# Two attention layers with a feed-forward on one core: another order of transposes in three places, weight pieces split earlier, and query and key tiles issued from ScalarE's queue

## The reference

```
layer 0:  q = x Wq^T, k = ctx Wk^T, v = ctx Wv^T
          att = softmax(q k^T / sqrt(32)) v
          x = x + att[0]                 # sequence 0 alone, added to all eight
layer 1:  xq = layer_norm(x), y = layer_norm(ctx)
          o = softmax(q k^T / sqrt(32)) v     # q from xq; k, v from y
          x = x + o Wproj + bproj
          h = gelu(layer_norm(x) W1 + b1)     # 512 -> 2048
          x = x + h W2 + b2
```

## Time and profile before

| | us |
|---|---|
| median of 3 runs (lowest, highest) | 1790.82 (1788.2, 1792.63) |
| profiled execution | 1793.32 |
| its span | 1791.5 |
| first score matmul of layer 1's passes: second, third, fourth | 490.3, 641.9, 806.5 |
| last product with values of the eighth pass begins the tail | 1626.4 |

### The profile page before, as it was taken

How to read it: one execution, slowest core, us unless ns; L and a number is a source line. 1 busy time by engine, 2 the same in 40 slices (tenths; PEclk the granted TensorE clock), 3 DMA queues, 4 the chain that set the end, 5 groups by cost and what they waited for, 6 DMA issues and landing times.

```text
span 1791.5 us, 23794 instructions
## 1 busy us (share of the span) xinstructions
PE 1714.7 (96%) x7456; PEld 1313.6 (73%) x7456; DVE 1082.1 (60%) x1865; ACT 1156.1 (65%) x1940; POOL 939.3 (52%) x802
## 2 busy tenths in 40 slices
PE   7899998998989999999999999999999999999999
PEld 5677776765666777777777777777777777777787
DVE  5565654477776666665666665666656666654322
ACT  4777764587877765765766577657657665775231
POOL 0444455157675564656465564646664655646341
PEclk9999999999999999999999999999999999999999
DMA  8789978674545675676676566756766775668262
GB/s 285 251 278 302 330 275 322 229 213 164 188 132 162 184 201 138 179 235 162 160 219 195 143 168 185 200 133 179 235 168 157 219 197 142 171 185 274 93 234 79
DMA packets 160077, 356.78 MB, mean 199 GB/s; under 512 B 29392, under 2 KB 50000, under 8 KB 159312
## 3 DMA queue, kind: packets, MB, share of 16 engines
q1 hardware_dynamic: 109072, 189.31, 35.8%
q10 hardware_dynamic: 50880, 165.95, 29.5%
HBM read 253.61 MB, written 82.08 MB: 187 GB/s over the span
## 4 chain that ended last, share of the span: by engine, by line
PE 69%; ACT 8%; DMA 7%; DVE 5%; issue 4%; POOL 3%; SPq 2%; ACTq 0%; DVEq 0%; POOLq 0%
PE ps_d L887 46%; PE ps_o L908 11%; PE ps_t L940 6%; PE ps_s L925 5%; DMA q_st<-negmax_t 3%; ACT p_hi L1054 2%; DVE negmax L1212 1%; DMA rs<-o_raw 1%; ACT ps_d L960 1%; ACT ps_t L1061 1%; ACT ht L1016 1%; POOL p_lo L1324 1%; SPq L728 1%; PE ps_d L815 1%; DMA v_scratch<-v_out 1%
## 5 line engine op out<-in xcount | busy, mean ns | idle before, releaser
L1324 POOL TENSOR_TENSOR p_lo<-p_full,p_hi 128x512 fp32r<-128x512 f32 x288 | 372.1, 1292 | 586.5 <-ACT p_full L1061 586.0
L1054 ACT ACTIVATE p_hi<-ps_t 128x512 fp32r<-128x512 f32 x576 | 345.7, 600 | 358.5 <-PE ps_t L940 355.0
L1212 DVE TENSOR_REDUCE negmax<-ps_s 128x1 fp32r<-128x512 f32 x576 | 388.9, 679 | 128.2 <-PE ps_s L925 127.6
L887 PE MATMUL ps_d<-hT,w_r 128*128 128x512 f32 x1536 | 419.0, 393 | 2.0 <-DVE hT L1109 2.0
L887 PE MATMUL ps_d<-w_r,g_s 128*128 128x512 f32 x1536 | 389.4, 393 | 0.0
L887 PEld LDWEIGHTS ps_d<-hT,w_r 128*128 128x128 f32 x1536 | 288.6, 189 | 73.7 <-DVE hT L1109 5.7
L887 PEld LDWEIGHTS ps_d<-w_r,g_s 128*128 128x128 f32 x1536 | 290.3, 189 | 64.6
L1225 DVE TENSOR_TENSOR p_lo<-ps_t,p_hi 128x512 fp32r<-128x512 f32 x288 | 198.8, 690 | 229.9 <-ACT ps_t L1061 229.2
L908 PE MATMUL ps_o<-p_hi,v_s 128*65 128x512 f32 x576 | 231.5, 402 | 14.7 <-POOL p_lo L1324 8.1
L940 PE MATMUL ps_t<-q_st,k_st 97*128 97x512 f32 x576 | 232.2, 403 | 11.6 <-DMA q_st<-negmax_t 10.9
L925 PE MATMUL ps_s<-k_st,q_st 96*128 96x512 f32 x576 | 231.8, 402 | 8.4 <-DVE negmax L1212 6.6
(11 more groups left out here) (102 smaller groups left out, 2160.6 us busy)
## 6 DMA issues: line engine op xcount, KB each, us to landing
w_r<-w_scratch ACTq DMA_DIRECT2D x214, 512.0 KB, 5.3
w_r<-w_scratch SPq DMA_DIRECT2D x42, 512.0 KB, 4.7
v_scratch<-v_out SPq DMA_DIRECT2D x36, 520.0 KB, 5.2
k_scratch<-kq_out SPq DMA_DIRECT2D x36, 512.0 KB, 4.9
q_st<-q_scratch SPq DMA_DIRECT2D x144, 128.0 KB, 4.5
k_st<-k_scratch SPq DMA_DIRECT2D x144, 128.0 KB, 4.3
o_ab<-o_raw SPq DMA_DIRECT2D x144, 128.0 KB, 3.5
w_scratch<-piece_out SPq DMA_DIRECT2D x16, 1024.0 KB, 6.4
```

Source lines behind the costliest of these rows:

```text
L887: ins = nc.tensor.matmul(bank(u), lhs[a], rhs[b], start=(i == 0 and m == 0), stop=(i == 3 and m == 2))
L1054: act.activation(p_hi[:, c], ps_t[:, c % 2], ACT.Exp, scale=SCALE)
L1212: dve.tensor_reduce(negmax[:, h % 2, c:c + 1], ps_s[:, c % 2], AX.X, ALU.max, negate=True).then_inc(s_maxed, 1)
L1324: pool.tensor_tensor(p_lo[:, c], p_full[:, (by_gpsimd(s) - 1) % 2], p_hi[:, c].bitcast(F32), ALU.subtract).then_inc(p_pool_split, 1)
```

## The change

- `keys_values` gives the same units in another order: the transposes of the next sequence come between the keys and values two at a time, and all of them ahead of the last value and the last key with its value. This holds in the first pass and in the gap.
- In the tail, the last `y2` unit of the sequence before goes ahead of the four `ht` transposes, where it stood between the second and the third.
- In the later passes the two `y2` units behind the second Gelu burst get three ticks of their own (25 to 27), and the four `ht` transposes with the hidden units the twelve after them, where all were spread over fifteen.
- The eight pieces of W2 are loaded, split and stored six ticks earlier.
- From tick `base[2]` on, ScalarE issues the heads' query and key tiles (after the exponentials and the emptying of its tick), SyncE no longer does. The waits ahead of them are the same.

```diff
--- before.py
+++ after.py
@@ -113,10 +113,9 @@
 
         def keys_values(b):
             units = []
-            for c in range(4):
-                units += [("k", b + 1, c), ("v", b + 1, c)]
-                if b + 1 < B:
-                    units.append(("a", 3 + b, c))
+            turns = [("a", 3 + b, c) for c in range(FC) if b + 1 < B]
+            units = [("k", b + 1, 0), ("v", b + 1, 0), *turns[:1], ("k", b + 1, 1), *turns[1:2], ("v", b + 1, 1), *turns[2:3],
+                     ("k", b + 1, 2), *turns[3:], ("v", b + 1, 2), ("k", b + 1, 3), ("v", b + 1, 3)]
             return units
 
         early = [("a", 2, c) for c in range(FC)]
@@ -174,8 +173,8 @@
                 spread([drain + 1], second(old, 2)[2:], front=True)
                 spread([drain + 2], second(old, 3)[:1], front=True)
                 spread([drain + 3], outs, front=True)
-                spread([drain + 4], second(old, 3)[1:3], front=True)
-                spread([drain + 5], turns[:2] + second(old, 3)[3:] + turns[2:], front=True)
+                spread([drain + 4], second(old, 3)[1:], front=True)
+                spread([drain + 5], turns, front=True)
                 spread([drain + 6], hidden(new, 0), front=True)
                 by_chunk(drain + 6, new, 0)
                 spread([drain + 7], hidden(new, 1), front=True)
@@ -197,7 +196,8 @@
                 spread(range(at + 22, at + 24), hidden(old, 3)[3:])
                 burst(at + 24, old, 3, second(old, 2)[:2])
                 rest = second(old, 2)[2:]
-                spread(range(at + 25, at + 40), rest + turns + hidden(new, 0))
+                spread(range(at + 25, at + 28), rest)
+                spread(range(at + 28, at + 40), turns + hidden(new, 0))
                 burst(at + 40, new, 0, second(old, 3)[:2])
                 spread(range(at + 41, at + 55), second(old, 3)[2:] + hidden(new, 1))
             else:
@@ -328,7 +328,7 @@
 
 
 def piece_tick(i):
-    return PRE + 19 + 5 * i if i < PIECES // 2 else PLAN.gap - 11 + 2 * (i - PIECES // 2)
+    return PRE + 19 + 5 * i if i < PIECES // 2 else PLAN.gap - 17 + 2 * (i - PIECES // 2)
 
 
 PIECE_SPLIT = listed([(piece_tick(i), i) for i in range(PIECES)])
@@ -369,6 +369,7 @@
 
 
 SHARED_FROM = PLAN.base[1] + 2
+STACKS_FROM = PLAN.base[2]
 
 HEADS, ROWS, PLACES, VALUES, STORES, STAGE_LOADS, RES_LOADS, OUT_STORES = sync_tables()
 
@@ -698,6 +699,22 @@
         queue.wait_ge(evacuated, ready("y2", n, 12 + t))
         queue.dma_start(rows(out, n - 1)[:, t], xres[n % 2][:, t]).then_inc(out_stored[n % 2], 16)
 
+    def load_stack(queue, h):
+        n, g, k = h // NH, h % NH // G, h % G
+        own = slice(h % NH * DK, h % NH * DK + DK)
+        if h >= G:
+            queue.wait_ge(t_ready, (h - G) * TC + TC)
+        elif h == 0:
+            queue.wait_ge(first_split["ctx0t"], FC)
+        if k == 0:
+            for u in (("k", n, g), ("q", n, g)):
+                i = KQ_NO[u]
+                queue.wait_ge(kq_stored[i % 2], 16 * (i // 2 + 1))
+        k_hi = kd[n, own, 0].unsqueeze(1).broadcast_to([DK, 2, T])
+        for dst, src in ((q_st[0:2 * DK, k], qd[n, own]), (k_st[0:2 * DK, k], k_hi),
+                         (q_st[2 * DK:KQ, k], qd[n, own, 0]), (k_st[2 * DK:KQ, k], kd[n, own, 1])):
+            queue.dma_start(dst.bitcast(F32), src).then_inc(stack_loaded[k], 16)
+
     def load_wo(queue):
         queue.wait_ge(unit_ready, ready("a", 10, FC - 1))
         queue.dma_start(wo_raw[:], wo).then_inc(wo_loaded, 16)
@@ -706,22 +723,6 @@
 
     @block.sync
     def _(sp):
-        def load_stack(h):
-            n, g, k = h // NH, h % NH // G, h % G
-            own = slice(h % NH * DK, h % NH * DK + DK)
-            if h >= G:
-                sp.wait_ge(t_ready, (h - G) * TC + TC)
-            elif h == 0:
-                sp.wait_ge(first_split["ctx0t"], FC)
-            if k == 0:
-                for u in (("k", n, g), ("q", n, g)):
-                    i = KQ_NO[u]
-                    sp.wait_ge(kq_stored[i % 2], 16 * (i // 2 + 1))
-            k_hi = kd[n, own, 0].unsqueeze(1).broadcast_to([DK, 2, T])
-            for dst, src in ((q_st[0:2 * DK, k], qd[n, own]), (k_st[0:2 * DK, k], k_hi),
-                             (q_st[2 * DK:KQ, k], qd[n, own, 0]), (k_st[2 * DK:KQ, k], kd[n, own, 1])):
-                sp.dma_start(dst.bitcast(F32), src).then_inc(stack_loaded[k], 16)
-
         def load_row(h):
             sp.wait_ge(max_turned, h + 1)
             for c in range(TC):
@@ -777,8 +778,8 @@
             early = tick < SHARED_FROM
             for u in STORES.get(tick, []) if early else ():
                 store(sp, *u)
-            for h in HEADS.get(tick, []):
-                load_stack(h)
+            for h in HEADS.get(tick, []) if tick < STACKS_FROM else ():
+                load_stack(sp, h)
             for h in PLACES.get(tick, []):
                 place_head(h)
             for n, g in VALUES.get(tick, []) if early else ():
@@ -1063,6 +1064,8 @@
                 move_head(weighted // TC)
             for u in EVACUATED.get((tick, True), []):
                 evacuate(*u)
+            for h in HEADS.get(tick, []) if tick >= STACKS_FROM else ():
+                load_stack(act, h)
             for n, group, c in G_HALVES.get(tick, []):
                 done = GELU_NO[n, group]
                 if (n, group) in PLAN.by_chunk.get(tick, []):
```

## The result

The change makes the kernel slower: 1814.6 us median (1813.54 to 1816.09) beside 1791.72 for the kernel before on the same chip, a ratio of 1.0108 (95% interval 1.0086 to 1.0131), or +19.4 us (15.4 to 23.5). The two medians lie 22.9 us apart; the ratio, with its interval, is what is used here. The forecast was 1783.4, faster, within 1774 to 1793.

A forecast was written before the change was run, and what follows sets the result against it. TensorE was taken as the bound, working 1714.7 of 1791.5 us, leaving 77 us to win. The terms summed to -7.4 us: 1785.9 for the profiled execution, 1783.4 against the median, range 1774 to 1793.

The forecast's parts named there:

- ScalarE issues the tiles: From head 34 on: issues hidden under ScalarE's exponentials, +1 us where ScalarE is full (490 to 520), bounds 0 and 8.
- the rival of ScalarE's sequencer: After Gelu bursts and at third pass's start: four issues push the next exponential, holding matmuls; +5.6 us, 1796, chance 0.07.
- Rows: SyncE's row copies no longer stand behind the tiles: -2 of their 3.2 us of waits, bounds -3.2 and +3.
- The queues hold each other up: Rival: SyncE's row issues wait for ScalarE's, rows come 2 us later; +8.6 us, 1799, chance 0.04.
- Turns: Later passes: transposes' wait goes, but ScalarE's emptying delays hidden units and splits; +0.5 a pass, +3 us, bounds -7.6 and +8.
- Pieces: W2 pieces six ticks earlier: gain at most 2.27 us, loss at most 4.5 from late splits; taken as +0.5.
- Terms (a) to (c): Gap: wait at 275.78 shortened, -1.5 and -0.7; wait at 309.37 gone, -6.4; new accumulator-reuse waits, +1.5; together -7.1 us.
- (c): Gap: value units reuse a chunk's accumulator after one large unit, waiting half a us and about 1 us; +1.5, bounds 0 and 2.9.
- the rival of the gain given back: Second layer reached 7 us sooner, but SyncE's queue or stores there set the pace; -0.3 us, 1790.5, chance 0.22.
- First pass and tail: First pass: 1.81 us wait at 137.98 goes, -1.8; tail: last output unit ahead of transposes, -1, bounds -3 and +1.7.

The follow-up runs named there:

- the issues alone: The kernel before with ScalarE issuing the query and key tiles from the second pass of the second layer on, nothing else: ratio 1.0098, +17.6 us.
- the turns alone: The kernel before with the two output units ahead of the transposes in the later passes, nothing else: ratio 1.0039, +7.0 us.
- two issues moved: The kernel before with ScalarE issuing the query tiles alone, two DMAs a head; SyncE keeps the key tiles: ratio 0.9985, -2.7 us.
- the four copies: The kernel before with ScalarE additionally issuing four 2 KB copies a head that nothing reads; SyncE keeps the tiles: ratio 1.0172, +31 us.
- the new order and tail: The kernel before with the new order of keys, values and transposes and the new tail, without the other three edits: ratio 0.9958, -7.5 us.
- the row early: The kernel before with new key order and tail, plus SyncE issuing the first pass's last head's output and row-of-sums copies two ticks earlier: ratio 0.9937.
- the pieces early: The kernel before with the last eight pieces of W2 six ticks earlier, nothing else: ratio 1.0018, +3.2 us.

## Why the prediction was wrong

**The step that failed** is "ScalarE issues the tiles", with its "hidden" and +1 us; issues and rows together measured +17.6 in place of -1. Its mechanism was written down as the rival of ScalarE's sequencer, but with a chance of 0.07, and mis-sized twice. The issue was priced at 0.33 to 0.51 us from one row each; the trace of before already had 0.58 and 0.60 us as medians of its 576 tile issues on SyncE, and on ScalarE four took 2.35 us with no pause (914.60). And that was held against the average distance of two exponentials, 2.5 us. By that measure 2.35 us would still have been hidden, so the price alone was not what failed. A tick's ScalarE work is not its two exponentials: the parts of the Gelu stand behind the issues in the same tick, `o_raw` in the next one, and other issues (weights, x) as well; at 807.61 six of them last 3.6 us. The row at the earlier trace rows, one issue of 0.33 us under one exponential, was read as proof for four. The rival's bounds (16 heads, six bursts) gave 1796; instead every pass from the third on lost 2.2 to 3.6 us with the issues alone. Two of the signs that the prediction named for being wrong came: an exponential behind the issues starts late (811.30), and the late passes are longer by more than 1.5 us.

**Rows.** -2 was forecast for SyncE's rows. Their wait, 3.2 us before, is 2.2 in the kernel after and 1.2 with the issues alone, but 1.9 with the turns alone too, where SyncE kept the tiles: what the term is worth is not shown. With two issues moved, the kernel is 2.7 us faster, not told apart from none.

**The queues hold each other up.** No support: the waits for the rows did not grow where ScalarE issues four in a tick (2.2, 1.2, and 3.0 with the four copies, against 3.2), and SyncE's four row issues beside ScalarE's took 2.2 us at 808.17 and at 914.96, as at the earlier trace rows.

**Turns.** +3 forecast, with bounds of -7.6 and +8; +7.0 (3.8 to 10) measured. That the wait would not go but move, to the hidden unit and the other transposes, was right; 0.5 us a pass was too little.

**Pieces.** +0.5 forecast, up to 4.5; +3.2 (0.2 to 6.5) measured. What was named as late next, the deviation on GpSimd and ScalarE's scaling behind it, is what the trace shows at 238.83 and 240.60. Missing was the row of sums in the crowded queue.

**The gap.** Terms (a) to (c) came to -7.1. The waits named did shrink or go: in the kernel after 309.37 is gone, the third transpose's went from 2.03 to 1.63. What failed, by the profiles, is (c), at +1.5. It took the inversion at 285.70 for VectorE's order alone, which would move up with TensorE; but the row of sums landed only 1.07 us ahead of it, and with the new order and tail no sooner (285.93). This is the rival of the gain given back, but in the gap itself, on SyncE's order of issues. With the row early the stretch was 8.2 us shorter than before in the profile, 5.4 us shorter than the shortest of the seven kernels with the old order. The times do not refute the sum: for first pass, gap and tail together -9.9 was forecast, and -7.5 (-10.4 to -4.8) measured.

**First pass and tail.** The first pass's wait of 1.81 us is gone, its worth is within what profiles differ there. The tail took 163.5 us in place of 165.1, with -1 forecast. But nine kernels with the old tail take 163.4 to 165.5 there, five with the new one 162.6 to 163.5: the sign fits, the size is not shown.

The parts add up: 17.6 + 7.0 + 3.2 - 7.5 = +20.3, and +19.4 was measured. The four intervals taken together leave some 6 us either way, so this is a coarse check.

## What to carry to other kernels

An engine that issues DMAs pays for them in its own order of instructions: count all issues of a tick end to end, and hold them against the room ahead of the first instruction behind them, not against the average pace. Where they do not fit, split them over ticks or queues; two a tick were free here, four cost 17.6 us. Before a wait is taken off an accumulator, ask for every engine in the chain whether it is held by its order or by a transfer: a small copy behind large stores does not come sooner because the matmuls do.

## What the runs showed of the hardware

An issue holds its sequencer for the whole of the time that the profile gives it: `o_raw` began at 917.73, 0.11 us after the last issue ended at 917.62, while an exponential handed over before ran on beside the issues. The Trainium skill, Perfetto Trace Analysis, section DMA Instruction — HWDGE, says that the end in the profile is the moment when the sequencer is free for the next instruction; these rows agree.

VectorE's copy at 233.67 took 1.25 us beside GpSimd's cast with the pieces early; with the new order and tail alone, when GpSimd had nothing in hand, it took 0.42. The cast, then the shorter copy:

```profile
233.60 1.04 POOL L1258 CAST piece_out<-w_raw 128x1024 fp32r<-128x1024 f32 x1
```

```profile
230.42 0.42 DVE L1180 COPY rs_t<-rinv 128x512 f32<-128x512 f32 x1
```

The long copy ended at 234.92, 0.28 us behind the cast (233.60 + 1.04). The fourteen traces of this case hold 504 of these copies. The 108 that began while GpSimd was idle took 0.41 to 0.43 us. Of the 396 that began inside one of its instructions, 376 ended 0.28 or 0.29 us behind the end of that instruction, whatever its length. The other 20 took 0.42 to 0.43 us: 16 began within 0.02 us of GpSimd's start, four in its last 0.08 us.

The Trainium skill, SBUF — State Buffer, section SBUF: two separate sides, says that VectorE and GpSimd share a pair of ports that, for some of VectorE's instructions, one of them holds for a whole instruction while the other waits. These copies agree with it.

With the new order and tail, the row of 2 KB took ten us from issue to landing in the gap (275.90 to 285.93), where the busy share of the DMA engines reads 1.05 from 274 to 287. It took 7.0 us at that place in the kernel before; the median of the 144 rows of that run is 4.25.
